# One TensorE signal a step for turned rows, turned inner values and results, and fewer signals in later pairs' attention

## What is computed

```python
h = tok(x, W, b, pos_embed)                       # 16 x 1024 x 64
h = h + attn(layernorm(h), Wk, bk, Wq, bq, Wv, bv, Wr, br)
# attn: softmax of K over the tokens, of Q within a head; ctx = K V^T; att = ctx Q
h = h + ffn(layernorm(h), gate_w, gate_b, w1, w2, w3)
# ffn: top 2 of 16 by softmax(x gate_w + gate_b); silu(x w1[e]) * (x w2[e]) @ w3[e]
```

## Time and profile before

| | |
|---|---|
| median of three runs | 795.47 us |
| the profiled execution | 794.0 us, of which the span of the profile is 792.1 us |
| busy: PE, POOL, DVE, ACT | 577.0, 518.1, 443.1, 347.6 us |
| indirect DMAs issued by POOL | 256 scatters of 997 ns, 224 + 32 gathers of some 950 ns |
| expert groups, tiles of a group | 96, 4 |

### The profile page before, as it was taken

How to read it: one execution, slowest core, us unless ns; L and a number is a source line. 1 busy time by engine, 2 the same in 40 slices (tenths; PEclk the granted TensorE clock), 3 DMA queues, 4 the chain that set the end, 5 groups by cost and what they waited for, 6 DMA issues and landing times.

```text
span 792.1 us, 14179 instructions
## 1 busy us (share of the span) xinstructions
PE 577.0 (73%) x3844; PEld 479.5 (61%) x3844; DVE 443.1 (56%) x1237; ACT 347.6 (44%) x753; POOL 518.1 (65%) x540
## 2 busy tenths in 40 slices
PE   5867668787899989898889988998959702973000
PEld 3455536585688668867786778686848702873000
DVE  5655653656556776776667567756755601454111
ACT  2233122152546466646564666456626701674111
POOL 2051077366771777777777777777777777777774
PEclk9987875597999999999999899989969965997555
DMA  2599032233463375528442844374344414544121
GB/s 78 111 243 388 1 96 82 71 106 94 129 186 84 78 177 146 150 54 199 135 136 55 201 128 122 75 180 115 107 117 128 113 51 123 139 101 98 40 40 30
DMA packets 168871, 93.20 MB, mean 118 GB/s; under 512 B 99680, under 2 KB 152928, under 8 KB 168800
## 3 DMA queue, kind: packets, MB, share of 16 engines
q1 hardware_dynamic: 151632, 66.71, 32.0%
q0 software_dynamic: 16384, 25.20, 11.7%
q10 hardware_dynamic: 784, 0.39, 0.2%
HBM read 45.06 MB, written 47.19 MB: 116 GB/s over the span
## 4 chain that ended last, share of the span: by engine, by line
PE 33%; POOL 26%; DVE 16%; issue 13%; DMA 6%; ACT 4%; POOLq 0%; ACTq 0%; DVEq 0%; SPq 0%
POOL sums L504 13%; POOL rows_scratch L487 9%; PE wide_ps L1013 6%; PE h_ps L1145 4%; PE y_ps L1162 3%; DMA hx<-xi_scratch 3%; DMA xi_scratch<-xi 2%; POOL hx L504 2%; POOL kexp L504 2%; PE turn_ps L1129 2%; DVE twice_y L953 2%; PE wide_ps L1105 2%; PE wide_ps L1033 2%; PE hidT_ps L1155 1%; PE wide_ps L1019 1%
## 5 line engine op out<-in xcount | busy, mean ns | idle before, releaser
L487 POOL DMA_INDIRECT rows_scratch<-z_parts,place x256 | 255.2, 997 | 128.7 <-issue 77.5
L504 POOL DMA_INDIRECT sums<-y_scratch,place x224 | 213.9, 955 | 83.6 <-issue 67.1
L1145 PE MATMUL h_ps<-w_hi,rowsT 128*128 x384 | 112.6, 323 | 39.3 <-DVE hid_all L955 34.0
L953 DVE SCALAR_TENSOR_TENSOR twice_y<-tanh,h_ps 128x256 f32<-128x256 f32 x192 | 79.6, 414 | 108.0 <-ACT tanh L601 90.1
L1145 PEld LDWEIGHTS h_ps<-w_hi,rowsT 128*128 128x128 f32 x384 | 75.5, 197 | 53.8 <-issue 52.4
L1162 PE MATMUL y_ps<-w_sb,hidT_all 128*128 x768 | 102.6, 279 | 1.0 <-ACT twice_y L614 1.0
L1145 PE MATMUL h_ps<-w_lo,rowsT 128*128 x384 | 101.5, 291 | 0.0
L1162 PEld LDWEIGHTS y_ps<-w_sb,hidT_all 128*128 128x128 f32 x768 | 99.1, 202 | 2.1 <-issue 2.1
L601 ACT ACTIVATE tanh<-h_ps 128x256 f32<-128x256 f32 x192 | 69.8, 386 | 63.7 <-PE h_ps L1145 58.5
L1129 PE MATMUL turn_ps<-ident,rows_all 128*128 128x128 f32 x384 | 62.5, 288 | 47.7 <-DMA rows_all<-rows_scratch 40.8
L955 DVE SCALAR_TENSOR_TENSOR hid_all<-twice_y,h_ps 128x256 f32<-128x256 f32 x192 | 80.7, 420 | 6.6
(11 more groups left out here) (250 smaller groups left out, 907.1 us busy)
## 6 DMA issues: line engine op xcount, KB each, us to landing
rows_all<-rows_scratch SPq DMA_DIRECT2D x96, 256.0 KB
y_scratch<-twice_y SPq DMA_DIRECT2D x96, 128.0 KB
rows_scratch<-tanh SPq DMA_DIRECT2D x3, 3072.0 KB, 19.5
xi_scratch<-xi SPq DMA_DIRECT2D x16, 256.0 KB, 3.4
rows_scratch<-z_parts,place POOLq DMA_INDIRECT x256
hx<-xi_scratch SPq DMA_DIRECT2D x14, 256.0 KB
sums<-y_scratch,place POOLq DMA_INDIRECT x224
out<-sums SPq DMA_DIRECT2D x56, 64.0 KB
```

The lines of the kernel that those rows point to most:

```text
L487: gp.indirect_dma_start(rows_dram[n], bass.IndirectOffsetOnAxis(ap=place[m % RING][:, r, j:j + 1], axis=0), z_parts[m % 2][:, j // 2, j % ...
L504: gp.indirect_dma_start(y_of[r][apart(m)][:, j // 2, j % 2, :], None, y_dram[m % 3], bass.IndirectOffsetOnAxis(ap=place[m % RING][:, r, j: ...
L953: ve.scalar_tensor_tensor(twice[:, j, :], tanh[:, j, :], 1.0, halves[:, j, 0, :], ALU.add, ALU.mult).then_inc(S["twice_done"], 1)
L1145: mm = te.matmul(h_ps[:, j * 256:(j + 1) * 256], rowsT[g % 2][:, j * P:(j + 1) * P], w[:, bass.ds(experts[g][j], 1), :, :].rearrange("d a ...
```

## The change

PE keeps one semaphore for the experts, `step_done`, raised by one at the end of `project_out(g-2)`, once a step (in the first two steps with groups, at the end of `turn`). Everyone who waited for turned rows, turned inner values or results now waits for the count of the step in which that work is done. ACT copies the inner values of a group one step later, and ahead of `copy_y` instead of after the tanh. For pairs 3 to 7 the embedding is signalled once for both images, queries and values once for two quarters, and the attention once for its three parts.

```diff
+        def rows_turned(groups):
+            return groups
+        def inner_turned(groups):
+            return groups + 3 if groups > 0 else 0
+        def projected(groups):
+            return groups + 4 if groups > 0 else 0
...
             def load_rows(g):
-                wait(sp, "rowsT_ps_ready", g - 2)
+                wait(sp, "step_done", rows_turned(g - 2))
...
                 if 0 <= s - LAG < GROUPS_ALL:
-                    wait(pool, "rowsT_ps_ready", min(s - LAG + 2, GROUPS_ALL))
+                    wait(pool, "step_done", rows_turned(min(s - LAG + 2, GROUPS_ALL)))
...
             def turn(g):
-                wait(act, "rowsT_ps_ready", g + 1)
+                wait(act, "step_done", rows_turned(g + 1))
...
             def copy_hidT(g):
-                wait(act, "hidT_ps_ready", g + 1)
+                wait(act, "step_done", inner_turned(g + 1))
...
-                wait(act, "y_done", g - 1)
+                wait(act, "step_done", projected(g - 1))
...
             def copy_y(g):
-                wait(act, "y_done", g + 1)
+                wait(act, "step_done", projected(g + 1))
...
                 if 0 <= g + 1 < GROUPS_ALL:
                     turn(g + 1)
+                if 0 <= g - 2 < GROUPS_ALL:
+                    copy_hidT(g - 2)
                 if 0 <= g - 3 < GROUPS_ALL:
                     copy_y(g - 3)
...
                 if 0 <= g < GROUPS_ALL:
                     activate(g)
-                if 0 <= g - 1 < GROUPS_ALL:
-                    copy_hidT(g - 1)
...
             def multiply(g):
-                wait(dve, "hidT_ps_ready", g - 1)
+                wait(dve, "step_done", inner_turned(g - 1))
...
-                                  start=False, stop=True).then_inc(S["emb_ps_ready"], 1)
+                                       start=False, stop=True)
+                        if m < 3:
+                            mm.then_inc(S["emb_ps_ready"], 1)
+                    if m >= 3:
+                        mm.then_inc(S["emb_ps_ready"], 2)
...
-                mm.then_inc(S["qv_ps_ready"], 1)
+                if m < 3:
+                    mm.then_inc(S["qv_ps_ready"], 1)
+                elif r % 2 == 1:
+                    mm.then_inc(S["qv_ps_ready"], 2)
...
-                        mm.then_inc(S["att_ps_ready"], 1)
+                        if m < 3:
+                            mm.then_inc(S["att_ps_ready"], 1)
+                    if m >= 3:
+                        mm.then_inc(S["att_ps_ready"], 3)
...
                 if 0 <= g + 2 < GROUPS_ALL:
-                    turn(g + 2)
+                    mm = turn(g + 2)
                 if 0 <= g - 2 < GROUPS_ALL:
-                    project_out(g - 2)
+                    mm = project_out(g - 2)
+                if 0 <= g + 2 < GROUPS_ALL + 4:
+                    mm.then_inc(S["step_done"], 1)
```

More of the change, by code:

```diff
@@ L266, in vit_kernel @@
             past_ready owner_ps_ready owner_ready ranked place_summed place_ready
-            rowsT_ps_ready rowsT_ready h_done tanh_done twice_done hid_done hidT_ps_ready hidT_ready y_done y_ready
+            step_done rowsT_ready h_done tanh_done twice_done hid_done hidT_ready y_ready
             part_ready gated_ready result_ready""".split()
@@ L482, in scatter @@
                     if m >= 3:
-                        wait(pool, "rowsT_ps_ready", GROUPS * (m - 2))
+                        wait(pool, "step_done", rows_turned(GROUPS * (m - 2)))
                     else:
@@ L1018, in embed @@
                     for b in range(2):
-                        te.matmul(wide_ps[:, b * 512:(b + 1) * 512], ident[:, :], pos_in[:, :, :].rearrange("p t e -> p (t e)"),
-                                  start=False, stop=True).then_inc(S["emb_ps_ready"], 1)
+                        mm = te.matmul(wide_ps[:, b * 512:(b + 1) * 512], ident[:, :], pos_in[:, :, :].rearrange("p t e -> p (t e)"),
+                                       start=False, stop=True)
[3 more added lines that the diff above has]
+                        mm.then_inc(S["emb_ps_ready"], 2)
             def queries(m, r):
@@ L1129, in turn @@
                     mm = te.transpose(turn_ps[:, j * P:(j + 1) * P], rows[g % 3][:, j, :, :].rearrange("p n e -> p (n e)"), ident[:, :])
-                mm.then_inc(S["rowsT_ps_ready"], 1)
+                return mm
             def project_in(g):
@@ L1155, in turn_hidden @@
                     mm = te.transpose(hidT_ps[:, j * P:(j + 1) * P], hid[g % 2][:, j, :], ident[:, :])
-                mm.then_inc(S["hidT_ps_ready"], 1)
             def project_out(g):
@@ L1163, in project_out @@
                                    w3_sb[:, bass.ds(e, 1), :].rearrange("h a d -> h (a d)"), start=True, stop=True)
-                mm.then_inc(S["y_done"], 1)
+                return mm
             setup_first()
```

## The result

The changed kernel takes 837.39 us (median of 4 runs, 832.20 to 841.19); the kernel before, with a fourth run added to its three, takes 794.83 us. The ratio is 1.053, with an interval of 1.046 to 1.060: 42.6 us or 5% slower, where 4.7 us or 0.6% had been forecast. The direction was right, the loss is nine times the forecast, and the time lies far outside the range of 796.5 to 806 us.

The account below looks back on a forecast made before the run. POOL alone was taken to set the time from step 38 on. Delays before it, 0.83 + 1.4 + 0.6 + 0.9 + 0.9, called 4.7 us with a small wait, gave 800.2 us on the median; range 796.5 to 806 us.

Parts of the forecast that it names:

- The bound of before: From 253.70 us, the start of step 38 on POOL, to the end, POOL's indirect DMAs alone set the time.
- second rival: Each pair costs over 7 us more, perhaps 12 steps paying 0.48 each, so POOL waits again; 806 to 810 us, chance 0.11.
- ACT's order: ACT's copies, now ahead of the tanh, delay DVE in three steps before POOL's step 38: +1.4 us, between 0 and 5.8.
- the room is used up: PE's 75.1 us a pair exceeds POOL's 82, POOL waits in steps 42 to 44 and later pairs; 806 to 810 us, chance 0.11.
- the signs that the prediction names for being wrong: POOL's start moving under 2 or over 8 us, POOL gaps in steps 42 to 44 or before later scatters, transposes under 0.11 us.
- the signal: POOL's wait before step 38 ends with `project_out` and not `turn`: +0.83 us.
- embedding: Pair 3: with one signal ACT's first square starts later and the second comes one square later, +0.6 us, lower bound 0.4.
- keys: Pair 3, step 32: ACT's exponential stands behind all three copies, starting 1.30 us after PE's step instead of 0.41, +0.9 us.
- queries: Pair 3, step 33: DVE gets both quarters only at 232.18 us, two operations of 0.46 us each later, +0.9 us.
- the 0.6, 0.9, 0.9 and 1.2 of the attention side: Added to each pair by embedding, keys, queries and attention; with ACT's order 80 to 81 us, still under POOL's 82.
- POOL's room: How long POOL's next work is ready beforehand: narrowest 2.91 us at step 42, some 1.7 us forecast to stay.
- The signal's own cost: On PE's transposes and product with w3, a signal costs at most 0.01 us, so fewer signals were taken to gain nothing.

Follow-up runs that it names:

- inner values back: The changed kernel with the inner values signalled and copied on ACT as before, against the kernel before: 795.99 us, ratio 1.003.

## Why the prediction was wrong

**The bound of before** was read rightly. The spans less POOL's start are 538.4, 538.0 and 538.9 us for the kernel before, its second profile and the one with inner values back, and no gap of POOL in them is over 0.32 us, so there POOL alone sets the time after step 38.

**The step that failed** is the second rival's ground together with "ACT's order". The prediction followed the moved copy only to ACT's tanh, and said that "most of those steps are PE's own"; it never named who waits for the copy itself. The text ahead of it names one that does, `project_out(g)`, the reader of the copy. But the copy also frees `hidT_ps`: there are two tiles `hidT` in SBUF and only one `hidT_ps` in PSUM, so `turn_hidden` waits for the copy too. The copy had most of a step of room ahead of `turn_hidden`, and no transpose waited for it; moved by one step and put behind the step's end it has none. With ACT free (step 32) the copy ends at 224.06 us, 1.13 us after the end of PE's step before, and PE's eight products of `project_in` are done a little sooner, so PE waits 0.27 us; wherever ACT is late, the lateness goes onto PE. The term was taken at 1.4 us before step 38, with 5.8 us as its bound, and 1 to 1.5 us a pair afterwards. The runs show 17 us for the moved copy alone, 62.6 us of waits in the whole change, 9.6 of them before step 38, and 31.9 us back when only the waiting transposes are moved.

**The rival "the room is used up"** is what happened, with a chance of 0.11. Its condition was over 7 us a pair, and it is 88.9 - 75.1 = 13.8 us. Its ground, 12 copies of 0.48 us a pair, was not what filled the room. The 7 us were also read off the shortest of four distances: the next three are 77.8 to 78.6 us before the change, with no wait of PE for rows from POOL in them, and only 3.4 to 4.2 us are left to POOL's 82. Its price of 806 to 810 us was too low, because only 1 to 2 us a pair had been allowed past the 7. Two of the signs that the prediction names for being wrong came: POOL's start moved by over 8 us (9.84), and POOL has gaps ahead of later scatters.

**The terms that were right.** In step 32 the exponential starts 224.21 - 222.93 = 1.28 us after PE's step ends (1.30 forecast). In step 33 DVE's four operations stand in a row after one wait of 2.31 us. The kernel with inner values back holds the signal, embedding, keys and queries, forecast at 0.83 + 0.6 + some 0.4 (the keys without the copy) + 0.9 = 2.7 us; measured is 1.003 of 794.33, 2.4 us (0.2 to 4.6), with POOL's start at 257.54, 3.8 us later than in the profile of before. That agrees within what these runs can tell; no term was measured by itself.

**"The change adds to each pair the 0.6, 0.9, 0.9 and 1.2 of the attention side"**, covered by POOL's room: it holds for the kernel with inner values back, though only just. Its 13 steps take 79.9, 83.5, 83.6 and 81.9 us, 82.2 on the mean, 4.7 more than before (77.5) and as much as POOL needs. (The prediction's own sum, 75.1 + 3.6 + 1 to 1.5, is 79.7 to 80.2 and not 80 to 81.) In the changed kernel the same edit costs 835.5 - 814.4 = 21 us, or 22 us by the ratios 1.055 and 1.027, since the two medians are from two chips. Nearly half of it lies before step 38, so the lost cover explains only the rest; the prediction had neither the cost without the cover nor the effect on the new wait.

**The signal's own cost** of at most 0.01 us is borne out by the rows: in a step without attention, four transposes without a signal and the product with w3 start 0.44 us apart in the changed kernel (643.38 and 643.82 us), just as with a signal before. No gain from fewer signals shows in a run that was repeated. What the Trainium skill ("TensorE: Matmul & The Clock Gate", section "The cost: per-tile semaphore tail") would give back if its figure held here, an estimated 0.8 us, is too small to see beside the run-to-run scatter, and these matmuls don't run side by side; no run here tests it alone.

## What to carry to other kernels

When a copy out of PSUM moves, list two waiters, the one that reads the copy and the one that writes the tile again, and look up how many buffers each side has. A copy made later costs nothing where there is slack, and all of the copying engine's lateness where there is none; moving the instruction that waits (here `turn_hidden`, by two places) can return most of what that lost, here 31.9 of 41.7 us. Costs that are hidden behind another engine's room share that room, and they can lengthen each other's waits: price each also as if the others had used the room up, and read the room at every pair, not at the first.

## What had not been expected of the hardware

The same program with the same inputs took 794 us on two chips and 1000 us on a third, in all 26 runs of the kernel before on the latter (995.3 to 1011.1). For the kernel with only the copy moved, profiled on both kinds of chip, the busy times of DVE, ACT and POOL are the same (447.5, 339.7 and 517.9 us, against 445.0, 338.0 and 518.7). PE's are not: 681.8 against 588.2 us, at a granted clock of 0.77 against 0.86. The rest of the loss was in gaps before instructions, which the profile puts down to issue or to "another core or an unknown queue" (18% of the chain in that run). The three variants run on both kinds kept their order, but not their sizes (1.042 and 1.027 for the change with the attention signals of before). Neither the cause nor whether the lower clock is part of it or follows from the gaps is known from these runs.
